# Four projections of a conditioned attention block: one plain float32 product in place of three split ones

## The reference

```
h      = gamma * layernorm(x) + beta          # gamma, beta from cond @ Wg.T, cond @ Wb.T
q,k,v  = h @ Wqkv.T + bqkv                    # 16 heads of 16 channels
att    = softmax(q @ k.T) / 16 ; out = att @ v
out    = out @ Wp.T + bp
h1     = out + x
result = (gamma * layernorm(h1) + beta) + h1
```

## Time and profile before

| | us |
|---|---|
| median of 3 runs | 348.88 (348.82 to 350.72) |
| time of the profiled execution | 349.5 |
| its span in the profile | 347.7 |
| TensorE busy | 334.0 (96%) |
| VectorE busy | 297.0 (85%) |
| ScalarE busy | 242.8 (70%) |
| GpSimd busy | 159.0 (46%) |

### The profile page before, as it was taken

The page is one execution under the profiler, slowest core; times in us unless marked ns, Lnnn a source line. Parts: engine busy times, 40 slices in busy tenths (PEclk is TensorE's granted clock), DMA queues, the critical chain, the costliest instruction groups (busy, mean ns, idle before and its releaser), DMA issues.

```text
span 347.7 us, 8982 instructions
## 1 busy us (share of the span) xinstructions
PE 334.0 (96%) x3173; PEld 288.6 (83%) x3173; DVE 297.0 (85%) x728; ACT 242.8 (70%) x476; POOL 159.0 (46%) x187
## 2 busy tenths in 40 slices
PE   8886989999999999999999999999999999999993
PEld 4675968889898888888898888888898888888773
DVE  4874877789898989989898989989898988998684
ACT  7762686868678686868687686868687686766740
POOL 5476261525464462726454462726454453225330
PEclk9997899999999999999999999999999999999999
DMA  8487245544555465565545565656546454652011
GB/s 239 128 202 204 58 123 151 150 134 129 161 131 158 135 180 155 136 173 139 157 133 156 134 176 153 141 154 160 156 135 154 106 170 124 168 147 75 18 60 60
DMA packets 47705, 48.87 MB, mean 141 GB/s; under 512 B 6287, under 2 KB 41374, under 8 KB 47662
## 3 DMA queue, kind: packets, MB, share of 16 engines
q1 hardware_dynamic: 44782, 47.00, 49.3%
q0 software_dynamic: 1984, 0.51, 0.9%
q10 hardware_dynamic: 896, 0.80, 0.8%
HBM read 9.99 MB, written 4.23 MB: 41 GB/s over the span
## 4 chain that ended last, share of the span: by engine, by line
PE 86%; DVE 5%; ACT 2%; DMA 2%; POOL 2%; issue 2%; SPq 0%; DVEq 0%; POOLq 0%; ACTq 0%
PE m L969 24%; PE st L969 19%; PE sa L969 18%; PE pv L969 17%; PE pv L1058 4%; PE pv L1139 2%; PE m L1098 2%; DMA wqkv<-WqkvT_dram 2%; DVE mx L688 1%; DVE qk_l L723 1%; POOL qk_l L415 1%; POOL xn L378 1%; PE pv L1072 1%; PE m L1072 1%; ACT qk_h L522 0%
## 5 line engine op out<-in xcount | busy, mean ns | idle before, releaser
L688 DVE TENSOR_REDUCE mx<-sa 128x2 f32<-128x512 f32 x256 | 171.6, 683 | 30.1 <-PE sa L969 29.0
L602 ACT ACTIVATE p<-st 128x512 f32<-128x512 f32 x240 | 140.9, 598 | 38.0 <-PE st L969 33.9
L969 PE MATMUL sa<-kst,qst 126*128 126x256 f32 x512 | 106.5, 290 | 1.6 <-DVE mx L688 1.1
L969 PE MATMUL st<-qst,kst 128*128 128x256 f32 x496 | 104.0, 292 | 0.7 <-DMA qst<-m_l 0.5
L969 PEld LDWEIGHTS st<-qst,kst 128*128 128x128 f32 x496 | 75.1, 188 | 14.3 <-issue 12.8
L969 PEld LDWEIGHTS sa<-kst,qst 126*128 126x128 f32 x512 | 80.0, 193 | 3.8 <-DVE mx L688 2.1
L369 POOL DMA_DIRECT2D qst<-m_h x31 | 17.6, 566 | 117.0 <-DVE m_l L697 117.0
L969 PE MATMUL pv<-p,v_st 128*32 128x256 f32 x1008 | 61.0, 382 | 0.0
L969 PEld LDWEIGHTS pv<-p,v_st 128*32 128x32 f32 x1008 | 29.5, 109 | 21.0 <-ACT p L602 1.8
L969 PE MATMUL m<-hT_h,wqkv_h 128*128 128x256 f32 x128 | 36.8, 300 | 1.4 <-issue 0.8
L378 POOL TENSOR_SCALAR xn<-xa,mv,rstd 128x256 f32<-128x256 f32 x28 | 34.2, 1227 | 1.4
(11 more groups left out here) (149 smaller groups left out, 568.3 us busy)
## 6 DMA issues: line engine op xcount, KB each, us to landing
qst<-qk_h SPq DMA_DIRECT2D x64, 128.0 KB, 2.4
qst<-qk_l SPq DMA_DIRECT2D x64, 128.0 KB, 2.5
kst<-qk_l SPq DMA_DIRECT2D x64, 128.0 KB, 2.7
kst<-qk_h SPq DMA_DIRECT2D x62, 128.0 KB, 2.4
xa<-x_dram SPq DMA_DIRECT2D x16, 256.0 KB, 3.0
gb<-gb_rows SPq DMA_DIRECT2D x16, 256.0 KB, 3.9
out_dram<-y SPq DMA_DIRECT2D x15, 256.0 KB, 3.4
wqkv<-WqkvT_dram SPq DMA_DIRECT2D x1, 512.0 KB, 5.8
```

The source lines that it names most:

```text
L602: nc.scalar.activation(p32[:, h, :], st_ps[h % 2][:], ACT.Exp).then_inc(exp_done, 1)
L688: dve.tensor_reduce(mx[:, par(a), h // HH, (h % HH) * TT:(h % HH + 1) * TT], sa_ps[h % 2][:].rearrange("p (t n) -> p t n", t=TT), AX.X, AL ...
L969: return nc.tensor.matmul(o, l, r, start=start, stop=stop)
```

## The change

All operands of the projections stay unsplit. `hT` and `aT` are plain float32, a quarter is one plain float32 product of `wqkv` and `hT` (or `aT` and `wp`), and every split of weights, h and attention rows is gone, with its semaphores. ScalarE makes `hT` of later sequences directly in its final place; in the opening ScalarE and VectorE make one half each. The quarters stand in pairs: q in slots 0, 0, 1, 1, k in 4, 4, 5, 5, the output projection in 12, 12, 13, 13; v stays in 7, 7, 8, 8. `project_first` and `project_second` are replaced by plain quarters. In step -1 the turning of x of sequence 2 moves from slot 8 to slot 10, and GpSimd normalises it before it makes the low part of k of sequence 1, not after. Of the warming products with zeros, five and one are left out at two places, and `warm_up_rows` adds eight plain products with 32 rows of ones, two on each quarter of the array's rows. In `last_step` and `finish` the same holds for the last output projections.

```diff
-Q_SLOTS, K_SLOTS, V_SLOTS, P_SLOTS = (0, 1, 3, 4), (4, 5, 5, 6), (7, 7, 8, 8), (12, 13, 14, 15)
+Q_SLOTS, K_SLOTS, V_SLOTS, P_SLOTS = (0, 0, 1, 1), (4, 4, 5, 5), (7, 7, 8, 8), (12, 12, 13, 13)
-WARM = (10, 4, 4, 4)
+WARM = (5, 3, 4, 4)
-X_FIRST = 8
+X_FIRST = 10
...
 # GpSimd, step -1
                     if first(b + 1) and h == 0:
                         low_full(1, 0, ql_ready)
+                        rstd_x(2)
+                        norm_x(2)
                     if first(b + 1) and h == 5:
-                        rstd_x(2)
                         low_full(1, 1, kl_ready)
-                        norm_x(2)
-                        pool.wait_ge(wph_ready, 1)
-                        pool.tensor_tensor(wp_l[:], wp[:], wp_h[:], ALU.subtract).then_inc(wpl_ready, 1)
...
-                    if h == 12:
-                        low_h(b + 3)
...
-            pool.wait_ge(wvh_ready, 1)
-            pool.tensor_tensor(wqkv_l[:, :, 2 * D:3 * D], wqkv[:, :, 2 * D:3 * D], wqkv_h[:, :, 2 * D:3 * D],
-                               ALU.subtract).then_inc(wvl_ready, 1)
...
 # ScalarE, h of later sequences, and the opening
-                nc.scalar.activation(hT_h[:, par(a)], hT[:], ACT.Copy).then_inc(hTh_ready, 1)
+                for k in range(KT):
+                    o = nc.scalar.activation(hT[:, par(a), k, :], m0[:, k * N:(k + 1) * N], ACT.Identity,
+                                             bias=bfull[:, k, a:a + 1], scale=gfull[:, k, a:a + 1])
+                o.then_inc(h_act, 1)
...
-            act.wait_ge(wqk_in, 16)
-            nc.scalar.activation(wqkv_h[:, :, 0:2 * D], wqkv[:, :, 0:2 * D], ACT.Copy).then_inc(wqkh_ready, 1)
             high_h_direct(0)
...
 # VectorE
-                    (11, 0): [lambda: low_max(b + 1, 0), lambda: low_att(b - 1), lambda: residual(b - 2, 5)],
+                    (11, 0): [lambda: low_max(b + 1, 0), lambda: residual(b - 2, 5)],
...
-            low_h_direct(0)
-            dve.wait_ge(wqkh_ready, 1)
-            dve.tensor_tensor(wqkv_l[:, :, 0:2 * D], wqkv[:, :, 0:2 * D], wqkv_h[:, :, 0:2 * D],
-                              ALU.subtract).then_inc(wqkl_ready, 1)
...
 # TensorE
-            def parts(o, l_h, l_l, r_h, r_l, k):
-
-                for n, (l, r) in enumerate(((l_h, r_h), (l_l, r_h), (l_h, r_l))):
-                    last = mm(o, l, r, k == 0 and n == 0, k == KT - 1 and n == 2)
-                return last
...
-                o = parts(ps[:, g * N:(g + 1) * N], wqkv_h[:, k, c:c + P], wqkv_l[:, k, c:c + P],
-                          hT_h[:, p, k, :], hT_l[:, p, k, :], k)
+                o = mm(ps[:, g * N:(g + 1) * N], wqkv[:, k, c:c + P], hT[:, p, k, :], k == 0, k == KT - 1)
...
+            def warm_up_rows():
+
+                pe.wait_ge(consts_ready, 1)
+                for _ in range(2):
+                    for j, bank in enumerate(last_st):
+                        mm(bank[:, 0:N], ones[32 * j:32 * (j + 1), 0:P], ones[32 * j:32 * (j + 1), :], True, True)
...
-                    for n, (a, w) in enumerate(((l[0], wp_h), (l[1], wp_h), (l[0], wp_l))):
-                        o = mm(ps, a, w[:, k, :], False, k == KT - 1 and n == 2 and (into == 0 or t == TT - 1))
+                    o = mm(ps, aT[:, k, t * P:(t + 1) * P], wp[:, k, :], False,
+                           k == KT - 1 and (into == 0 or t == TT - 1))
```

More of the change, by code:

```diff
@@ L574, in step @@
                         wait(act, proj_done, 1 * (b - 2) + 1)
-                        nc.scalar.activation(aT_h[:].rearrange("p k n -> p (k n)"), pv_ps[1][:],
-                                             ACT.Copy).then_inc(aTh_ready, 1)
+                        nc.scalar.activation(aT[:].rearrange("p k n -> p (k n)"), pv_ps[1][:],
+                                             ACT.Copy).then_inc(aT_ready, 1)
                     if h == S_VH and has(b + 1) and has(b - 1):
                         high_v(b + 1, m0)
[L579 to L586, removed]
                     if h == (X_FIRST if first(b + 1) else S_XT) + 1:
@@ L612, in high_h_direct @@
                 act.wait_ge(gfull_ready, 1)
[L613 to L618, removed]
+                nc.scalar.activation(hT[:, par(a), 0, :], st_ps[0][:, 0:N], ACT.Identity, bias=bfull[:, 0, a:a + 1],
+                                     scale=gfull[:, 0, a:a + 1]).then_inc(h_act, 1)
             def high_k0():
@@ L756, in h_direct @@
                 wait(dve, xnT_done, 1 * a + 1)
[L757 to L774, removed]
+                dve.tensor_scalar(hT[:, par(a), 1, :], st_ps[1][:, 0:N], gfull[:, 1, a:a + 1], bfull[:, 1, a:a + 1],
+                                  ALU.mult, ALU.add).then_inc(h_dve, 1)
             def residual(a, stage):
@@ L826, in last_high_att @@
                 wait(dve, proj_done, 1 * (a - 1) + 1)
[L827 to L832, removed]
-                dve.tensor_tensor(aT_l[:, k, :], bank[:, 0:N], aT_h[:, k, :], ALU.subtract).then_inc(aTtl_ready, 1)
+                dve.tensor_copy(aT[:].rearrange("p k n -> p (k n)"), pv_ps[1][:]).then_inc(aT_ready, 1)
             def normalise_half(c):
@@ L997, in project_out @@
                 t, k = quarter // KT, quarter % KT
-                o = parts(m1[:, t * D:(t + 1) * D], aT_h[:, k, t * P:(t + 1) * P],
-                          aT_l[:, k, t * P:(t + 1) * P], wp_h[:, k, :], wp_l[:, k, :], k)
+                o = mm(m1[:, t * D:(t + 1) * D], aT[:, k, t * P:(t + 1) * P], wp[:, k, :], k == 0, k == KT - 1)
                 if quarter == 3:
@@ L1041, in weigh @@
                 if g == 1:
-                    wait(pe, aTl_ready, 1 * b)
+                    wait(pe, aT_ready, 1 * b)
                 for q in range(2):
@@ L1163, in last_weigh @@
                 if half == 0:
-                    wait(pe, aTl_ready, B - 1)
+                    wait(pe, aT_ready, B - 1)
                 else:
@@ L1294, in step @@
                     for quarter in [n for n in range(4) if P_SLOTS[n] == h and has(b - 1)]:
-                        if quarter == 0 and first(b - 1):
-                            pe.wait_ge(wpl_ready, 1)
                         if quarter == 0:
-                            wait(pe, aTl_ready, 1 * (b - 1) + 1)
+                            wait(pe, aT_ready, 1 * (b - 1) + 1)
                             wait(pe, h1_ready, 1 * (b - 2) + 1)
@@ L1326, in _ @@
             warm_up(WARM[1])
-            pe.wait_ge(wqkh_ready, 1)
-            pe.wait_ge(hTh_ready, 1)
-            pe.wait_ge(gfull_ready, 1)
-            project_first()
+            pe.wait_ge(wqk_in, 16)
+            pe.wait_ge(h_act, 1)
+            pe.wait_ge(h_dve, 1)
+            for quarter in range(4):
+                project_qk(0, 0, m0, q_done, quarter)
+            for quarter in range(4):
+                project_qk(0, 1, m1, k_done, quarter)
             rows_gb()
@@ L1336, in _ @@
             pe.wait_ge(ql_ready, 1)
-            pe.wait_ge(hTh_ready, 2)
-            project_second()
+            pe.wait_ge(h_act, 2)
+            pe.wait_ge(h_dve, 2)
+            for quarter in range(4):
+                project_qk(1, 0, m0, q_done, quarter)
             steps(step)
```

93 lines of the change are left out of this document (16 added, 77 removed).

## The result

The changed kernel takes 366.17 us (median of 4 runs, 363.72 to 366.38), the kernel before 348.85 beside it: a ratio of 1.047, 95% interval 1.044 to 1.050. It is slower, by 17.3 us where 11.7 were forecast. That is inside the stated range (356.8 to 366.5), near its upper end, and outside the narrower range of the prediction's own case, which ended at 364. The profiled execution has a span of 364.4 us, 16.7 more than before.

The account below looks back on a forecast made before the run. TensorE was taken to bound the kernel from 58 to 293 us. Steps +16.6, late steps +0.6, end +0.1, opening -5.8, step 0 +0.2 make +11.7: 361.2 us profiled, forecast 360.6, 80% between 356.8 and 366.5.

Parts of the forecast that it names:

- the prediction's own case: Whole kernel: the forecast without its rivals, 360.6 us, own range 358 to 364; it kept 58%.
- the price of a quarter: Each projection quarter on TensorE: 0.433 us plain for 0.353 as three reduced products, so 0.080 more.
- nowhere in the ordinary steps: Ordinary steps: TensorE never waits for its maxima there; over the span only twice, 1.1 us in all.
- So no new wait, but the margin is small: Ordinary steps: pairing the quarters makes TensorE wait nowhere new, though slots 3, 6, 14 and 15 lose 0.35 of cover.
- The rival's 13 x 0.35 = 4.6: Slots 14, 15 and 3: bunched pairs starve TensorE by one 0.35 in every step, 365.5 us; 11%.
- Switching: Rival, all steps: changing between plain and reduced products costs 0.20 a pair, 22 us in all, 383 us; 2%.
- pass price: Rival, every quarter: a pass costs as much as a reduced product, so 0.117 a quarter, 369 us; 6%.
- (c): Step -1: column maxima transposed earlier, full clock without the pause, first `st` at 30.7 to 31; opening -5.8 us.
- (a): Opening: no rounding of the weights, q rounded 0.8 earlier, first `sa` at 19.8 for 20.66, -0.85 us.
- (b): Step -1: GpSimd's rows of sequence 2 ready at 25.0, not 28.8, so TensorE's 2.58 us of waiting go.
- The first rival: Opening gives only the pause back (clock falls again or SyncE's transfers hold everything): -2.6 for -5.8, 364 us; 15%.
- Step 0 and the end: Step 0 +0.2 us, from -0.8 to +1.0; after the main steps +0.6 (step 14, last step) and +0.1 (end).

Follow-up runs that it names:

- experiment 5: The kernel before with a fourth reduced product (low x low) in every quarter of the loop; 374.26 us, ratio 1.070.
- the reordered one: The kernel before with only GpSimd's new order and the turning in slot 10 of step -1; 345.62 us, again 344.34, ratio 0.987 both times.
- experiment 3: The changed kernel with the quarters unpaired, in the slots of the kernel before; 360.13 us, ratio 1.033.

## Why the prediction was right, and where its sizes were off

**The bound and the price of a quarter: right.** TensorE had no slack in an ordinary step, so its longer row showed in full (experiment 5 shows the same). A plain record is 0.217 from the next, a quarter 0.433. The step came to 20.83 where 20.78 were forecast, but as a sum of three terms of which the prediction had one. The price is +1.28; with the old slots the step is 20.64, 1.14 over 19.50, so about 0.14 came back, which the prediction had not; and the pairs add 0.2. Of the 0.14, 0.11 is a wait before one `sa` in slot 10 of the kernel before, by the spacing of its records: it is in every ordinary step of the kernel before and of the reordered one, and in none of the changed kernel, of experiment 3 or of experiment 5. The table of waits doesn't list it, so the prediction's "nowhere in the ordinary steps" missed it. Experiment 5 still has all the work of the splits, so it was not the relief of the other engines that closed this wait; the three kernels without it share the longer row of TensorE. Relief for the other engines bought nothing that shows, as the prediction had said.

**The pairs: underrated.** The prediction said "So no new wait, but the margin is small". It had checked the slots that lose cover against VectorE's maxima, at 3, 14 and 15; slot 6, which it listed too, was not followed to the next user of the bank. v in slot 7 waits there for VectorE's work on q in `m0`. The rival's 13 x 0.35 = 4.6 was nearly met in size, by another wait than the one it named: 0.2 in each of the eleven steps between the first and the last of the 13, 0.8 in step 0 and 0.8 at the end, some 3.5 to 4 in all.

**Switching, pass price: rightly small.** Experiment 3 excludes a price of switching, with 12 switches in a step in place of 8 and a shorter step. Experiment 5 excludes that a pass inside a plain product costs as much as a reduced product.

**The opening: right in its mechanisms, mis-sized by the clock.** The step that was mis-sized is "**-5.8 us.**" in (c), through (a) under it: (a) took TensorE's pace from 9 us on as that of the kernel before, and costed the left-out warming at nothing ("left out where TensorE waits anyway"). The first `sa` was forecast at 19.8 and came at 22.50, 2.7 late, and that is nearly all of the miss of 2.9; from it to the first `st` the prediction has 11.1 (19.8 to 30.9) and the trace 11.3, so (b) and (c) were right in size. The profile after has -2.9, since its clock was late; with an early clock it is -6.2 and -6.5. That the warming is to blame for the late clock is likely, not shown; that the late clock is what took the gain is shown.

The first rival gave 364 from "the clock falls again": the clock's price was there, but it did not fall later, it came later. By the prediction's own sign, a first `st` "near 34: the first rival", that rival was met; its other sign, the clock full throughout, could not be read from the clock column.

The wait for GpSimd's rows and the half clock behind it went as said. Undone in the changed kernel, that costs 3.2 us (with a half clock of 3.41); done alone in the kernel before, it moves the first `st` by 5.7 (there the half clock lasted 6.84). So the forecast was right that the opening gains, but nearly all of that gain belongs to GpSimd's order, which needs no plain products.

**Step 0 and the end** were forecast at +0.2 and +0.7 and came to +1.2 and +1.65; with the old slots the end is +0.8. So, by the marks, 2.9 of the 5.0 us that the span's sum is short are the opening, 1.0 is step 0, 0.95 the end and 0.15 the steps between. All four lie on the same side. That the time is still inside the stated range is owed to the two rivals that widened it, one right in size for the clock, the other in size for the pairs, and both by another cause than they named: that much is luck.

## What to carry to other kernels

A plain float32 product is four passes of TensorE in two records (0.433 us for 256 columns here); three reduced products are three passes (0.353). Replacing the split frees every other engine and is slower all the same where TensorE has no gap, so count passes before instructions. When a change brings a new order of other work along, as GpSimd's here, try that order alone: it was the part worth keeping. When a filler is moved out of a slot, ask of each following slot which bank it writes and who still reads it, not only whether the main loop keeps pace. And when two versions differ by about 1%, look at single times for groups before the median is explained: here one clock step in the opening is worth 2.6 us.

## What the runs showed of the hardware that was not expected

- The moment of the first full clock differs between executions of one program: the two profiles of the reordered kernel have it at 14.1 and at 5.5 us. Over all kernels it was 4.1 to 6.4 us or 13.9 to 14.4. In the late executions of the changed kernel TensorE was not idle for long in between; its records went on at half pace, 0.427 per plain record of 256 columns in place of 0.216.
- The profile's clock column shows 1.00 ahead of the first recorded change even where the spacing of the records is that of half the clock.
- A reduced product costs 0.1175 us in the loop with 256 columns, a pass inside a plain product 0.108. Why the first is dearer is open; weight loads last as long in both (0.19).
